# Second attention of a two-layer kernel: results of a batch carried by transfers into one array of full rows, divided once per batch, projected by one product per half

## The chip, the cores and the metric

The kernel runs on one core of a Trainium2 chip. A core has TensorE (PE, matrix products into PSUM), VectorE (DVE), ScalarE (ACT), GpSimd (POOL) and SyncE (SP), which in this kernel issues the transfers (DMAs); 16 DMA engines carry them. The metric is the time of one execution on the device in microseconds (us), as a median of several runs; lower is better.

## The reference

Two layers are computed on an input of 4 batches, 1024 tokens and 128 features: layer 0 (a scan, an attention, gated experts) and layer 1 (an attention over 16 heads of 8 features, then routed experts). The change touches the attention of layer 1 alone:

```python
h = NUM_HEAD                     # 16
hd = d_model // h                # 8
scale = jnp.sqrt(jnp.float32(h + D_KV + D_Q))      # 12
...
query = qt_c + qt_r
key = kt_c + kt_r
value = heads(ct_kv @ Wu_v_w + Wu_v_b)
attn = jnp.einsum('bhqd,bhkd->bhqk', query, key) / scale
attn = jax.nn.softmax(attn, axis=-1)
out = jnp.einsum('bhqk,bhkd->bhqd', attn, value)
out = out.transpose(0, 2, 1, 3).reshape(b, s, d_model)
return out @ Wo_w + Wo_b
```

## The kernel before, in words

The attention of layer 1 is the function `head_attention`; its tiles have names that begin with `h_`. It works in 16 groups n = 0 to 15 (`NGR`): 4 batches (`B`) of 4 groups (`NG`), and each group has 4 heads (`HG`). A group takes 16 steps i (`NI`): two halves of the 1024 queries (512 each, `CH`) by 8 tiles of 128 keys.

In a step TensorE makes two score tiles for two heads each (`scores`, line 1282, into `ps_st`), ScalarE takes their exponentials (`h_P`, line 1438), and one step later `values` (line 1292) multiplies them with the values into `ps_o`. The 4 heads of a group lie there at partitions 0, 32, 64 and 96; of each 32 partitions 9 are in use, 8 for the head's features and the ninth for the sum of the exponentials. `keep` (ScalarE, line 1404) copies each half to one of 7 arrays `o`.

The softmax needs each query's maximum. For it TensorE makes score tiles of another form in a ring of three PSUM banks (`maxima`, line 1266), two pairs of tiles a step and 24 pairs (12 steps) ahead of `scores`, and VectorE reduces each tile (line 1552): four reductions a step. After half a group the maxima are settled, GpSimd splits them into bf16 parts (`split`), TensorE turns them (`turn`, at steps 6 and 14), ScalarE keeps the turned rows (`h_m_row`, line 1397), and SP lays them beside the queries of the coming scores with four DMAs (`place_maxima`, line 1181). The scores of a half wait for these four (`m_landed`).

The division by the sums goes through memory. SP stores the four rows of sums (line 1186), loads them flat (1190), VectorE inverts them between two reductions (`invert`, line 1512), which falls at about step 8 of the group after, SP stores them (1194) and spreads each head's row over 32 partitions with four DMAs (line 1199, into `h_inv`). GpSimd multiplies `o` with `inv` (`norm`, line 1456), two instructions per group. When a batch's four groups are done, the output projection of its half c is four products accumulated over the groups (`output`, line 1249), with weights `h_Wo` padded with zeros for the 24 unused partitions of each head. These stand at step 2 of the third and fourth group of the next batch: two products ahead of the second pair of maxima of that step, two behind it. The last batch has its own way: sums spread by a product (line 1314), inverted on VectorE (1536, 1538), and `out_last` (line 1324), half 0 at step 13 of group 15, half 1 behind the last values.

SP is one queue in this order, for each n: `fetch_sums(n-1)`, `place_maxima(n, 1)`, in two groups of a batch `swap_rows`, then `spread_sums(n-1)`, in two groups of a batch `keep_parts` (768 KB of new keys or queries to memory), `load(n+2)` (12 DMAs of keys and queries, line 1754, 768 KB), and `place_maxima(n+1, 0)`. Between step 8 and step 14, groups n with n mod 4 of 0 or 1 also carry two products of the next batch's preparation (`product`, at steps 9 and 11); the others carry none. So `load` and the placing of the next group's maxima stand behind `spread_sums` on SP.

Of the kernel before, what the change touches and what calls it, by code (L numbers as in the profile page):

```python
# [1073 lines left out]
def head_weights(nc, ctx, S, A):  # L1074

    def sb(name, shape):
        return ctx.enter_context(nc.sbuf_tensor("h_" + name, shape, F32))

    W = S.head = State()
    W.Wd, W.bd, W.Wu, W.Wk, W.Wkv = sb("Wd", [D, 2, 64]), sb("bd", [128, 1]), sb("Wu", [64, 2, D]), sb("Wk", [D, D]), sb("Wkv", [128, 2, D])  # L1080
    W.Wo, W.bv, W.cos, W.sin = sb("Wo", [128, NG, D]), sb("bv", [128, NG]), sb("cos", [128, T]), sb("sin", [128, T])
    W.sums = sb("sums", [128, 128])
    W.loaded = semaphore(nc, ctx, "h_weights_loaded")
    W.count = 14


def load_head_weights(sp, S, A):

    W = S.head
    for to, x in ((W.Wd[:, 0, :], "Wd_q"), (W.Wd[:, 1, :], "Wd_kv"), (W.bd[0:64, :], "bd_q"), (W.bd[64:128, :], "bd_kv"),  # L1090
                  (W.Wu[:, 0, :], "Wq_r1"), (W.Wu[:, 1, :], "Wu_q"), (W.Wk[:, :], "Wk_r1"), (W.Wkv[64:128, 0, :], "Wu_k"), (W.Wkv[64:128, 1, :], "Wu_v"), (W.bv[:, :], "bvG"),
                  (W.cos[:, :], "cos1"), (W.sin[:, :], "sin1"), (W.sums[:, :], "sums_of")):
        sp.dma_start(to, A[x]).then_inc(W.loaded, 16)
    sp.dma_start(W.Wo[:, :, :], A["WoG1"].rearrange("p (g d) -> p g d", g=NG)).then_inc(W.loaded, 16)


def head_attention(nc, S, A):
# [8 lines left out]
    NB, PR, NBUF, NOB, NLOAD, MIX = 3, 4, 4, 7, 12, 16  # L1106
# [24 lines left out]
    with stage(nc) as ctx:  # L1131
        def sb(name, shape, dt=F32):
            return ctx.enter_context(nc.sbuf_tensor("h_" + name, shape, dt))

        def sem(name):
            return semaphore(nc, ctx, "h_" + name)
# [7 lines left out]
        o = [sb(f"o{i}", [128, T]) for i in range(NOB)]  # L1144
        inv = [sb(f"inv{i}", [128, T]) for i in range(2)]
# [75 lines left out]
        def _(pe):  # L1221
# [95 lines left out]
            def out_last(c, g0, g1):  # L1317
                for g in range(g0, g1):
                    n = (B - 1) * NG + g
                    if g == 0:  # L1320
                        pe.wait_ge(normed, 2 * (NGR - 1))
                    if g == NG - 1:
                        pe.wait_ge(normed_last, 2 * (c + 1))
                    last = pe.matmul(ps_max[:, 1 + c, :], Wo[:, g, :], o[n % NOB][:, c * CH:(c + 1) * CH], start=(g == 0), stop=(g == NG - 1))
                if g1 == NG:
                    last.then_inc(out_made, 1)

            pe.wait_ge(W.loaded, 16 * W.count)
            for g in range(NG):
                last = pe.matmul(ps_max[:, 0, 0:1], Wo[:, g, :], bv[:, g:g + 1], start=(g == 0), stop=(g == NG - 1))  # L1330
            last.then_inc(bias_made, 1)
# [8 lines left out]
            for n in range(NGR):  # L1340
                for i in range(NI):
# [12 lines left out]
                    if key and key[0] == "out":  # L1354
                        output(key, 0, NG // 2)
# [3 lines left out]
                    if key and key[0] == "out":  # L1359
                        output(key, NG // 2, NG)  # L1360
                    if n == NGR - 1 and i == KT + 1:
                        spread_last_sums(0)
                    if n == NGR - 1 and i == NI - 3:
                        out_last(0, 0, NG)
            values(NGR - 1, NI - 1)
            out_last(1, 0, 1)
            spread_last_sums(1)
            out_last(1, 1, NG)

        @block.scalar  # L1370
        def _(act):
# [79 lines left out]
        def _(pool):  # L1451
            def norm(n, c):
                cols = slice(c * CH, (c + 1) * CH)
                pool.wait_ge(inv_loaded, 16 * HG * (n + 1))
                pool.wait_ge(o_kept, 2 * n + 2)
                pool.tensor_tensor(o[n % NOB][:, cols], o[n % NOB][:, cols], inv[n % 2][:, cols], ALU.mult).then_inc(normed, 1)
# [21 lines left out]
            for n in range(NGR):  # L1478
# [3 lines left out]
                if n >= 2:  # L1482
                    for c in range(2):
                        norm(n - 2, c)
# [13 lines left out]
            for c in range(2):  # L1498
                norm(NGR - 2, c)

        @block.vector
        def _(dve):
# [1079 lines left out]
def layout(i):  # L2582
# [13 lines left out]
    def paired(a):  # L2596
# [30 lines left out]
        "Wu_k": paired(i["L1_attn_Wu_k_w"]), "Wu_v": i["L1_attn_Wu_v_w"], "bvG": beside(i["L1_attn_Wu_v_b"].reshape(NG, HG, 8), np.zeros((NG, HG, 24))).reshape(NG, 128).T,  # L2627
        "WoG1": beside(i["L1_attn_Wo_w"].reshape(NG, HG, 8 * D), np.zeros((NG, HG, 24 * D))).reshape(NG, 128, D).transpose(1, 0, 2).reshape(128, NG * D), "Wr": i["L1_ffn_Wr"], "b2": i["L1_ffn_b2"].reshape(1, X * D), "W1": i["L1_ffn_W1"], "W2": i["L1_ffn_W2"],
# [60 lines left out]
```

## Time and profile before

| | |
|---|---|
| median of 3 runs | 2175.93 us (2174.69 to 2179.72) |
| the profiled execution | 2174.7 us, its span 2172.9 us |
| busy over the span | PE 85%, DVE 67%, ACT 51%, POOL 31% |
| attention of layer 1, groups 0 to 15 | from about 1283 us to 1982 us of the span |

The busy shares are means over many stages; what a stage is bound by is read in that stage. In the timeline an entry merges equal instructions: the start, the time from the first start to the last end, the engine, the line, the operation, its tiles and shapes, the number of instructions, and in brackets the idle time ahead of it and what ended it. A product of f32 operands shows as two MATMUL entries, one of bf16 as one.

### The profile page before, as it was taken

Reading aid. Unit: us, or ns where it says so; the run is one execution under the profiler, and the core shown is the slowest. Engines: PE = TensorE matmul, PEld = TensorE weight load, DVE = VectorE, ACT = ScalarE, POOL = GpSimd, SP = SyncE. Lnnn points to the kernel's source line nnn. Section 1 sums busy time; section 2 is a strip of 40 time slices with the busy share of each in tenths; the row PEclk is TensorE's granted clock in tenths of the full one; section 3 lists DMA queues with packets and bytes.
Section 4 is the critical chain, followed back from the end, with each engine's and each line's share of the span. In section 5 each row is a group of like instructions: output and inputs, shape, how many; then the busy total and the mean of one; then the engine's idle time right before and its main releaser. Section 6 shows DMA issues by size and latency. Waiting matters only on the chain. (4 is left out here: it accounts for less than half of the span.)

```text
span 2172.9 us, 33046 instructions
## 1 busy us (share of the span) xinstructions
PE 1851.2 (85%) x12141; PEld 675.9 (31%) x12141; DVE 1464.0 (67%) x3100; ACT 1111.0 (51%) x1383; POOL 667.8 (31%) x804
## 2 busy tenths in 40 slices
PE   7454799999999999999499868888888888887879
PEld 3123233333333333333433312112211211113556
DVE  5864666666566566653344588999898899973443
ACT  4312244444444445444224248778777778774422
POOL 0032455544545465512025002403312511010052
PEclk9777799999999999999599969999999999998889
DMA  3000000000000000000021001101111111003114
GB/s 123 0 1 1 1 12 12 12 12 12 12 12 13 12 12 22 13 12 12 19 107 56 23 14 57 47 27 54 64 35 37 51 51 41 27 22 101 59 32 134
DMA packets 58229, 74.01 MB, mean 34 GB/s; under 512 B 23492, under 2 KB 39876, under 8 KB 57940
## 3 DMA queue, kind: packets, MB, share of 16 engines
q1 hardware_dynamic: 56500, 68.21, 10.0%
q0 software_dynamic: 1280, 2.62, 0.4%
q8 instruction: 98, 1.61, 0.3%
q10 hardware_dynamic: 288, 1.05, 0.2%
q14 instruction: 63, 0.52, 0.1%
HBM read 50.02 MB, written 16.98 MB: 31 GB/s over the span
## 5 line engine op out<-in xcount | busy, mean ns | idle before, releaser
L1552 DVE TENSOR_REDUCE h_m_half<-h_ps_max 128x1 f32<-128x512 f32 x1024 | 635.7, 683 | 66.7 <-PE h_ps_max L1266 64.2
L1438 ACT ACTIVATE h_P<-h_ps_st 128x1024 f32<-128x1024 f32 x512 | 496.9, 1022 | 93.1 <-PE h_ps_st L1282 90.3
L925 ACT ACTIVATE l_P<-l_ps_st 128x1024 f32<-128x1024 f32 (+3 forms) x384 | 306.8, 809 | 297.6 <-PE l_ps_st L808 296.5
L808 PE MATMUL l_ps_st<-l_Q,l_K 64*128 64x512 f32 (+3 forms) x1536 | 329.1, 509 | 0.4 <-DMA l_Q<-l_m_row 0.4
L1002 DVE CUSTOM_DVE_ANT_0 l_masked<-l_ps_t,l_mask 128x384 bf16<-128x384 f32 (+3 forms) x512 | 230.2, 487 | 83.0 <-PE l_ps_t L766 81.5
L1266 PE MATMUL h_ps_max<-h_K,h_Q 48*128 48x512 bf16 x1024 | 204.8, 396 | 91.7 <-DVE h_m_half L1552 89.9
L1292 PE MATMUL h_ps_o<-h_P,h_V 128*9 128x512 f32 x2048 | 269.2, 598 | 0.7 <-ACT h_P L1438 0.5
L1005 DVE TENSOR_REDUCE l_m_half<-l_ps_t 128x1 f32<-128x512 f32 x256 | 164.9, 686 | 100.6 <-PE l_ps_t L766 100.5
L973 POOL TENSOR_SCALAR_AFFINE_SELECT l_P<-l_P 128x256 f32<-128x256 f32 x256 | 103.2, 409 | 390.5 <-ACT l_P L925 390.0
L1282 PE MATMUL h_ps_st<-h_Q,h_K 51*128 51x512 bf16 x1024 | 169.3, 382 | 12.1 <-DMA h_Q<-h_m_row 4.9
L1469 POOL CAST h_m_parts<-h_m_neg 128x16 bf16<-128x16 f32 x32 | 6.3, 198 | 550.9 <-DVE h_m_neg L1529 550.9
L1266 PEld LDWEIGHTS h_ps_max<-h_K,h_Q 48*128 48x128 bf16 x1024 | 50.3, 93 | 399.6 <-DVE h_m_half L1552 376.5
L766 PE MATMUL l_ps_t<-l_Kh,l_Qh 64*128 64x512 bf16 (+3 forms) x768 | 129.7, 333 | 44.7 <-DVE l_m_half L1002 18.4
L823 PE MATMUL l_ps_o<-l_P,l_V 128*17 128x512 f32 (+3 forms) x1536 | 161.6, 493 | 6.2 <-POOL l_P L973 6.2
L808 PEld LDWEIGHTS l_ps_st<-l_Q,l_K 64*128 64x128 f32 x1536 | 127.4, 187 | 103.3 <-issue 46.8
L766 PE MATMUL l_ps_t<-l_Kl,l_Qh 64*128 64x512 bf16 (+3 forms) x768 | 128.0, 329 | 0.0
L766 PE MATMUL l_ps_t<-l_Kh,l_Ql 64*128 64x512 bf16 (+3 forms) x768 | 128.0, 329 | 0.0
L766 PEld LDWEIGHTS l_ps_t<-l_Kh,l_Qh 64*128 64x128 bf16 x768 | 37.6, 93 | 221.8 <-DVE l_m_half L1002 97.7
L944 POOL TENSOR_TENSOR l_t<-l_t,l_sin 128x512 f32<-128x512 f32 x72 | 92.3, 1282 | 37.8 <-DVE l_t L1023 37.8
L1022 DVE TENSOR_TENSOR l_t<-l_ps_t,l_cos 128x512 f32<-128x512 f32 x64 | 44.3, 691 | 66.2 <-PE l_ps_t L787 64.7
L950 POOL TENSOR_TENSOR l_Q<-l_t 128x512 f32<-128x512 f32 x64 | 81.8, 1278 | 8.4
L787 PE MATMUL l_ps_t<-xn,l_Wq 128*128 128x512 f32 x128 | 73.0, 654 | 4.2 <-DVE l_t L1023 4.2
(375 smaller groups left out, 2327.3 us busy)
## 6 DMA issues: line engine op xcount, KB each, us to landing
l_inv<-inverse_sums SPq DMA_DIRECT2D x60, 128.0 KB
h_inv<-inverse_sums SPq DMA_DIRECT2D x60, 128.0 KB, 2.8
y_rows<-zero SPq DMA_DIRECT2D x8, 512.0 KB, 4.9
h_b<-h_a SPq DMA_DIRECT2D x32, 128.0 KB, 2.0
c_W<-in_W SPq DMA_DIRECT2D x16, 256.0 KB, 5.6
c_back<-y_rows SPq DMA_DIRECT2D x16, 256.0 KB, 5.2
k_parts<-h_parts SPq DMA_DIRECT2D x4, 768.0 KB, 4.1
h_K<-k_parts SPq DMA_DIRECT2D x32, 96.0 KB
```

The costliest lines, as they stand in the source:

```text
L766: last = pe.matmul(tile(t + a)[:, 0:w], q[n % 2][rows, p, qt * 128:(qt + 1) * 128], k[n // NG % 2][rows, lo:lo + w], start=(x == 0), stop= ...
L808: last = pe.matmul(ps_st[x % 2][:, a, 0:w], K[n // NG % 2][rows, kt * 128:(kt + 1) * 128], Q[n % NQ][rows, c, p, q0 - c * CH:q0 - c * CH + ...
L823: last = pe.matmul(ps_o[32 * j:32 * j + M, q0 - c * CH:CH], V[n // NG][:, kt, :], P[(2 * (n * NI + i) + j // 2) % PR][:, j % 2, 0:w], star ...
L925: act.activation(P[e % PR][:, :, 0:w], ps_st[slot["s", n, i, p] % 2][:, :, 0:w], ACT.Exp, scale=0.125).then_inc(consumed, 1)
L973: pool.affine_select(P[e % PR][:, :, 0:128], P[e % PR][:, :, 0:128], [[0, 2], [1, 128]], ALU.is_ge, 0.0, base=0, channel_multiplier=-1).th ...
L1002: dve.tensor_tensor_reduce(out=masked[(t + a) % NB][:, 0:w], in0=ps, in1=mask[:, CH - w:CH], scale=-1.0, scalar=-NEG, op0=ALU.add, op1=ALU ...
L1005: dve.tensor_reduce(to, ps, AX.X, ALU.max, negate=True).then_inc(tile_freed, 1)
L1266: pe.matmul(ps_max[:, (t + a) % NB, :], Q[n % NBUF][rows, p, qt * 128:(qt + 1) * 128], K[n % NBUF][rows, p, lo:lo + CH], start=True, stop= ...
L1282: last = pe.matmul(to[:, a, :], K[n % NBUF][rows, p, kt * 128:(kt + 1) * 128], Q[n % NBUF][rows, p, c * CH:(c + 1) * CH], start=True, stop ...
L1292: last = pe.matmul(ps_o[32 * j:32 * j + M, :], V[b % 2][:, kt, g * HG + j, :], P[(2 * (n * NI + i) + j // 2) % PR][:, j % 2, :], start=(kt ...
L1438: act.activation(P[e % PR][:, :, :], ps_st[x % 2][:, :, :], ACT.Exp, scale=1.0 / 12.0).then_inc(consumed, 1)
L1552: dve.tensor_reduce(m_half[:, half, 2 * p + a, qt:qt + 1], ps_max[:, t % NB, :], AX.X, ALU.max, negate=True)\
```

## The change

A group's results are no longer divided where they stand. After the inverses of a group are stored, SP carries its 4 times 8 feature rows by four SBUF to SBUF DMAs into 32 rows of a new array `packed` (one of two, by the batch), which holds the 128 features of a whole batch in full rows; and it spreads each head's inverse over 8 partitions, not 32, at the same rows of `inv` (one per batch, no longer per group). GpSimd divides once per batch, two instructions, ahead of `split(2n+1)` in the second group of the batch after. The output projection of a half is one product of 128 full rows with the unpadded weights. Of the last batch the first three groups are divided that way (96 rows) and its fourth as before, so `out_last` has two products per half. Since `o` is free once it was carried, there are 4 arrays `o`, not 7; `keep` waits for the carries (`o_packed`) and for the stored sums of four groups back.

```diff
-    NB, PR, NBUF, NOB, NLOAD, MIX = 3, 4, 4, 7, 12, 16
+    NB, PR, NBUF, NOB, NLOAD, MIX = 3, 4, 4, 4, 12, 16
...
+        packed = [sb(f"packed{i}", [128, T]) for i in range(2)]
...
                 sp.wait_ge(inv_stored, 16 * (n + 1))
-                if n >= 2:
-                    sp.wait_ge(normed, 2 * (n - 1))
+                if n >= 2 * NG:
+                    sp.wait_ge(normed, 2 * (n // NG - 1))
+                    sp.wait_ge(consumed, item["out", n // NG - 2, 1] + 1)
+                if n:
+                    sp.wait_ge(o_packed, 16 * HG * n)
                 for j in range(HG):
-                    sp.dma_start(inv[n % 2][32 * j:32 * j + 32, :], inv1[n, j].partition_broadcast(32)).then_inc(inv_loaded, 16)
+                    at = 32 * (n % NG) + 8 * j
+                    sp.dma_start(packed[n // NG % 2][at:at + 8, :], o[n % NOB][32 * j:32 * j + 8, :]).then_inc(o_packed, 16)
+                for j in range(HG):
+                    at = 32 * (n % NG) + 8 * j
+                    sp.dma_start(inv[n // NG % 2][at:at + 8, :], inv1[n, j].partition_broadcast(8)).then_inc(inv_loaded, 16)
...
-            def output(key, g0, g1):
+            def output(key):
                 _, b, c = key
-                if g0 == 0:
-                    free_slot(item[key])
-                    pe.wait_ge(normed, 2 * NG * (b + 1))
-                for g in range(g0, g1):
-                    last = pe.matmul(ps_st[item[key] % 2][:, 0, :], Wo[:, g, :], o[(b * NG + g) % NOB][:, c * CH:(c + 1) * CH],
-                                     start=(g == 0), stop=(g == NG - 1))
-                if g1 == NG:
-                    last.then_inc(st_ready, 1)
+                to = free_slot(item[key])
+                pe.wait_ge(normed, 2 * (b + 1))
+                pe.matmul(to[:, 0, :], Wo[:, 0, :], packed[b % 2][:, c * CH:(c + 1) * CH], start=True, stop=True).then_inc(st_ready, 1)
...
+            def out_last(c, last):
+                cols = slice(c * CH, (c + 1) * CH)
+                if last:
+                    pe.wait_ge(normed_last, 2 * (c + 1))
+                    pe.matmul(ps_max[:, 1 + c, :], Wo[:, 1, :], o[(NGR - 1) % NOB][:, cols], start=False, stop=True).then_inc(out_made, 1)
+                else:
+                    pe.wait_ge(normed, 2 * B)
+                    pe.matmul(ps_max[:, 1 + c, :], Wo[0:96, 0, :], packed[(B - 1) % 2][0:96, cols], start=True, stop=False)
...
                 if n >= NOB:
-                    act.wait_ge(consumed, item["out", (n - NOB) // NG, 1] + 1)
+                    act.wait_ge(o_packed, 16 * HG * (n - NOB + 1))
+                    act.wait_ge(sums_stored, 16 * (n - NOB + 1))
...
-                if n >= 2:
+                if n % NG == 1 and n > NG:
                     for c in range(2):
-                        norm(n - 2, c)
+                        norm(n // NG - 1, c)
```

TensorE's queue at step 2 of a group that carries an `output`, before:

```order
L1292 MATMUL h_ps_o<-h_P,h_V 9x512 x4
L1249 MATMUL h_ps_st<-h_o,h_Wo 128x512 x2
L1266 MATMUL h_ps_max<-h_K,h_Q 128x512 x2
L1249 MATMUL h_ps_st<-h_o,h_Wo 128x512 x2
L1282 MATMUL h_ps_st<-h_Q,h_K 128x512 x2
L1266 MATMUL h_ps_max<-h_K,h_Q 128x512 x2
```

The same place in the changed program (the lines have moved by four):

```order
L1296 MATMUL h_ps_o<-h_P,h_V 9x512 x4
L1256 MATMUL h_ps_st<-h_packed,h_Wo 128x512
L1270 MATMUL h_ps_max<-h_K,h_Q 128x512 x2
L1286 MATMUL h_ps_st<-h_Q,h_K 128x512 x2
L1270 MATMUL h_ps_max<-h_K,h_Q 128x512 x2
```

Four products around a pair of maxima have become one product ahead of it. SP's queue in a group without `keep_parts`, from the store of the inverses on, before:

```order
L1194 DMA inverse_sums<-h_flat 128x32
L1199 DMA h_inv<-inverse_sums 32x1024 x4
L1754 DMA h_K<-k_parts 24x1x2048
L1754 DMA h_K<-k_parts 16x1x2048
L1754 DMA h_K<-k_parts 8x2048
...
L1181 DMA h_Q<-h_m_row 3x4x128 x4
```

And in the changed program:

```order
L1196 DMA inverse_sums<-h_flat 128x32
L1205 DMA h_packed<-h_o 8x1024 x4
L1208 DMA h_inv<-inverse_sums 8x1024 x4
L1755 DMA h_K<-k_parts 24x1x2048
L1755 DMA h_K<-k_parts 16x1x2048
L1755 DMA h_K<-k_parts 8x2048
...
L1183 DMA h_Q<-h_m_row 3x4x128 x4
```

Four DMAs now stand between the store of the inverses and the spread, so everything behind them, the 12 loads and the placing of the maxima, is issued four DMAs later.

## Rows read from the trace of the kernel before

**Rows 1.** Waits from 1290 to 1985 us: total in us, times, longest.

```profile
DVE h_m_half L1552 <- PE h_ps_max L1266: 52.0, 56, 1.9
...
PE h_ps_st L1282 <- DMA h_Q<-h_m_row: 4.9, 3, 2.0
```

**Rows 2.** VectorE's timeline at an output step (group 6, step 2).

```profile
1547.27 1.29 DVE L1552 TENSOR_REDUCE h_m_half<-h_ps_max 128x1 f32<-128x512 f32 x2 [1.90 <-PE h_ps_max L1266]
1549.72 1.29 DVE L1552 TENSOR_REDUCE h_m_half<-h_ps_max 128x1 f32<-128x512 f32 x2 [1.16 <-PE h_ps_max L1266]
1551.74 1.29 DVE L1552 TENSOR_REDUCE h_m_half<-h_ps_max 128x1 f32<-128x512 f32 x2 [0.73 <-PE h_ps_max L1266]
```

**Rows 3.** VectorE's timeline at a step with one product.

```profile
1304.56 2.48 DVE L1552 TENSOR_REDUCE h_m_half<-h_ps_max 128x1 f32<-128x512 f32 x4 [1.04 <-PE h_ps_max L1266]
1307.25 2.48 DVE L1552 TENSOR_REDUCE h_m_half<-h_ps_max 128x1 f32<-128x512 f32 x4 [0.20 <-PE h_ps_max L1266]
```

**Rows 4.** TensorE's timeline, one product (at 1303) and four (at 1544).

```profile
1303.08 1.13 PE L1233 MATMUL h_ps_st<-hT,h_Wd 128*128 128x512 f32 x2
...
1544.93 1.98 PE L1249 MATMUL h_ps_st<-h_o,h_Wo 128*128 128x512 f32 x4
```

**Rows 5.** Timeline of the last group, steps 8 to 14.

```profile
1955.86 2.50 POOL L1456 TENSOR_TENSOR h_o<-h_o,h_inv 128x512 f32<-128x512 f32 x2 [7.90 <-DMA h_inv<-inverse_sums]
...
1963.67 3.70 PE L1324 MATMUL h_ps_max<-h_o,h_Wo 128*128 128x512 f32 x8
...
1967.74 1.94 ACT L1438 ACTIVATE h_P<-h_ps_st 128x1024 f32<-128x1024 f32 x2 [3.58 <-PE h_ps_st L1282]
```

**Rows 6.** SP's timeline in group 7 (no product between steps 8 and 14).

```profile
1610.25 1.72 SPq L1199 DMA_DIRECT2D h_inv<-inverse_sums  x4
1612.07 3.77 SPq L1754 DMA_DIRECT2D h_K<-k_parts  x6
1615.88 3.68 SPq L1754 DMA_DIRECT2D h_Q<-q_parts  x6
1622.78 2.98 SPq L1181 DMA_DIRECT2D h_Q<-h_m_row  x4
```

**Rows 7.** SP's timeline in group 1 (two products between).

```profile
1349.11 4.41 SPq L1754 DMA_DIRECT2D h_K<-k_parts  x6
...
1361.30 3.01 SPq L1181 DMA_DIRECT2D h_Q<-h_m_row  x4
```

**Rows 8.** TensorE's timeline, first scores of groups 3 and 8.

```profile
1407.49 0.61 PE L1282 MATMUL h_ps_st<-h_Q,h_K 51*128 51x512 bf16 x4 [1.84 <-DMA h_Q<-h_m_row]
...
1627.06 0.60 PE L1282 MATMUL h_ps_st<-h_Q,h_K 51*128 51x512 bf16 x4
```

**Rows 9.** VectorE's timeline behind the wait of group 3.

```profile
1408.33 1.29 DVE L1552 TENSOR_REDUCE h_m_half<-h_ps_max 128x1 f32<-128x512 f32 x2 [1.36 <-PE h_ps_max L1266]
1410.38 2.68 DVE L1552 TENSOR_REDUCE h_m_half<-h_ps_max 128x1 f32<-128x512 f32 x4 [0.76 <-PE h_ps_max L1266]
```

**Rows 10.** Windows: time, PE, PEld, DVE, ACT, POOL busy, TensorE clock, DMA share, GB/s.

```profile
1390.00:1395.00 5.00, 4.30 (x36) 0.85 (x32) 5.00 (x9) 3.92 (x5) 0.00 (x0) 1.00 0.87 270
...
1406.40:1406.80 0.40, 0.00 (x0) 0.00 (x0) 0.40 (x1) 0.00 (x0) 0.00 (x0) 1.00 0.00 0
1408.00:1410.00 2.00, 2.00 (x14) 0.25 (x12) 1.29 (x2) 2.00 (x3) 0.00 (x0) 0.66 0.00 0
1614.00:1622.00 8.00, 6.88 (x54) 1.38 (x50) 7.96 (x15) 6.28 (x7) 2.97 (x6) 1.00 0.21 78
1625.40:1625.80 0.40, 0.27 (x2) 0.10 (x2) 0.40 (x2) 0.40 (x1) 0.00 (x0) 1.00 0.04 8
```

**Rows 11.** DMA issues on SP: count, duration ns min/median/max (three queries).

```profile
L1199 SPq DMA_DIRECT2D h_inv<-inverse_sums x60: 322/421/432, 1346.9 to 1952.8; - x60
...
L1703 SPq DMA_DIRECT2D h_b<-h_a x24: 517/591/1078, 1297.1 to 1695.4; - x24
...
L715 SPq DMA_DIRECT2D l_Q<-l_m_row x64: 634/641/823, 230.2 to 998.6; - x64
```

More of the change, by code:

```diff
@@ L1080, in head_weights @@
     W.Wd, W.bd, W.Wu, W.Wk, W.Wkv = sb("Wd", [D, 2, 64]), sb("bd", [128, 1]), sb("Wu", [64, 2, D]), sb("Wk", [D, D]), sb("Wkv", [128, 2, D])
-    W.Wo, W.bv, W.cos, W.sin = sb("Wo", [128, NG, D]), sb("bv", [128, NG]), sb("cos", [128, T]), sb("sin", [128, T])
+    W.Wo, W.bv, W.cos, W.sin = sb("Wo", [128, 2, D]), sb("bv", [128, 1]), sb("cos", [128, T]), sb("sin", [128, T])
     W.sums = sb("sums", [128, 128])
@@ L1093, in load_head_weights @@
         sp.dma_start(to, A[x]).then_inc(W.loaded, 16)
-    sp.dma_start(W.Wo[:, :, :], A["WoG1"].rearrange("p (g d) -> p g d", g=NG)).then_inc(W.loaded, 16)
+    sp.dma_start(W.Wo[:, :, :], A["WoG1"].rearrange("p (g d) -> p g d", g=2)).then_inc(W.loaded, 16)
 def head_attention(nc, S, A):
@@ L1166, in head_attention @@
         inv_stored, inv_loaded, normed, joined = sem("inv_stored"), sem("inv_loaded"), sem("normed"), sem("joined")
+        o_packed = sem("o_packed")
         block = ctx.enter_context(nc.Block())
@@ L1315, in spread_last_sums @@
                   .then_inc(spread_last, 1)
[L1317 to L1326, printed above, removed]
+            def out_last(c, last):
[6 more added lines that the diff above has]
+                    pe.matmul(ps_max[:, 1 + c, :], Wo[0:96, 0, :], packed[(B - 1) % 2][0:96, cols], start=True, stop=False)
             pe.wait_ge(W.loaded, 16 * W.count)
-            for g in range(NG):
-                last = pe.matmul(ps_max[:, 0, 0:1], Wo[:, g, :], bv[:, g:g + 1], start=(g == 0), stop=(g == NG - 1))
-            last.then_inc(bias_made, 1)
+            pe.matmul(ps_max[:, 0, 0:1], Wo[:, 0, :], bv[:, 0:1], start=True, stop=True).then_inc(bias_made, 1)
             pe.wait_ge(cleared, 1 + 2)
@@ L1354, in _ @@
                     if key and key[0] == "out":
-                        output(key, 0, NG // 2)
+                        output(key)
                     elif key:
@@ L1358, in _ @@
                     maxima(n + (s + 1) // NPAIR, (s + 1) % NPAIR)
-                    if key and key[0] == "out":
-                        output(key, NG // 2, NG)
                     if n == NGR - 1 and i == KT + 1:
@@ L1363, in _ @@
                     if n == NGR - 1 and i == NI - 3:
-                        out_last(0, 0, NG)
+                        out_last(0, False)
+                        out_last(0, True)
             values(NGR - 1, NI - 1)
-            out_last(1, 0, 1)
+            out_last(1, False)
             spread_last_sums(1)
-            out_last(1, 1, NG)
+            out_last(1, True)
         @block.scalar
@@ L1451, in _, with norm @@
         def _(pool):
[L1452 to L1456, printed above, removed]
+            def norm(b, c):
+                cols, hi = slice(c * CH, (c + 1) * CH), 128 if b < B - 1 else 96
+                groups = hi // 32 + NG * b
+                pool.wait_ge(inv_loaded, 16 * HG * groups)
+                pool.wait_ge(o_packed, 16 * HG * groups)
+                pool.tensor_tensor(packed[b % 2][0:hi, cols], packed[b % 2][0:hi, cols], inv[b % 2][0:hi, cols], ALU.mult).then_inc(normed, 1)
             def join(b):
@@ L1498, in _ @@
             for c in range(2):
-                norm(NGR - 2, c)
+                norm(B - 1, c)
         @block.vector
@@ L1534, in divide_last @@
                 if c == 0:
-                    dve.wait_ge(normed, 2 * (NGR - 2))
-                dve.reciprocal(inv[n % 2][:, cols], ps_max[:, 0, :]).then_inc(normed_last, 1)
+                    dve.wait_ge(normed, 2 * (B - 1))
+                dve.reciprocal(inv[B % 2][:, cols], ps_max[:, 0, :]).then_inc(normed_last, 1)
                 dve.wait_ge(normed_last, 2 * c + 1)
-                dve.tensor_tensor(o[n % NOB][:, cols], o[n % NOB][:, cols], inv[n % 2][:, cols], ALU.mult).then_inc(normed_last, 1)
+                dve.tensor_tensor(o[n % NOB][:, cols], o[n % NOB][:, cols], inv[B % 2][:, cols], ALU.mult).then_inc(normed_last, 1)
             def join_last(c):
@@ L2626, in layout @@
         "Wk_r1": paired(i["L1_attn_Wk_r_w"]),
-        "Wu_k": paired(i["L1_attn_Wu_k_w"]), "Wu_v": i["L1_attn_Wu_v_w"], "bvG": beside(i["L1_attn_Wu_v_b"].reshape(NG, HG, 8), np.zeros((NG, HG, 24))).reshape(NG, 128).T,
-        "WoG1": beside(i["L1_attn_Wo_w"].reshape(NG, HG, 8 * D), np.zeros((NG, HG, 24 * D))).reshape(NG, 128, D).transpose(1, 0, 2).reshape(128, NG * D), "Wr": i["L1_ffn_Wr"], "b2": i["L1_ffn_b2"].reshape(1, X * D), "W1": i["L1_ffn_W1"], "W2": i["L1_ffn_W2"],
+        "Wu_k": paired(i["L1_attn_Wu_k_w"]), "Wu_v": i["L1_attn_Wu_v_w"], "bvG": i["L1_attn_Wu_v_b"].reshape(D, 1),
+        "WoG1": beside(i["L1_attn_Wo_w"], beside(i["L1_attn_Wo_w"][96:].reshape(HG, 8 * D), np.zeros((HG, 24 * D))).reshape(128, D)), "Wr": i["L1_ffn_Wr"], "b2": i["L1_ffn_b2"].reshape(1, X * D), "W1": i["L1_ffn_W1"], "W2": i["L1_ffn_W2"],
         "fw1": i["L1_ffn_fw1"], "fw2": i["L1_ffn_fw2"],
```

## The prediction

> **What bounds the kernel now.** I read the waits of this attention first. VectorE waits for score tiles 52.0 us in 56 places, and TensorE waits 3 times, 4.9 us in all and at most 2.0, for the turned maxima that SP lays beside the queries [rows 1]. In ordinary steps VectorE never idles: its four reductions set the step, 2.48 us (the four in one row of [rows 3]). So TensorE's work costs only where it holds VectorE up, and SP's only where its DMAs land later than the scores want them. Its idles stand at the inserted products and behind those three waits. The timeline of VectorE shows an output step: 1.90 + 1.16 + 0.73 = 3.79 us [rows 2]. There are six (three batches, two halves), 22.7 of the 52.0 us. A step with one product ahead of its second maxima costs 1.04 + 0.20 = 1.24 us [rows 3].
>
> **What the output products give back.** TensorE's timeline has two products in 1.98 us before and again behind the maxima, and 1.13 us for a lone one [rows 4]. The change leaves one, at the place of the lone product of [rows 3]. So an output step should idle VectorE as that one does: 3.79 - 1.24 = 2.55 us less, six times 15.3 us. Bounds: if the 0.20 falls away, 16.5; TensorE itself loses three of four products, 3 x 1.98/2 = 3.0 us, so at most 17.8. I take 15.3. The eviction of the result is unchanged.
>
> In the last group four products of half 0 stand in ScalarE's way: 3.70 us of TensorE and 3.58 us of idle ScalarE [rows 5]. Two are left, 1.85 us saved, all of it from a wait that stays above it: 1.8 us. Of half 1 the removed products stood behind the last sums and in front of VectorE's division, in cover. Together **17.1 us** gained.
>
> **GpSimd** loses 22 of 30 divisions, each half of the pair in 2.50 us [rows 5]. It is off the path: nothing. At the end the division must still precede TensorE's products at 1963.67; it began at 1955.86 and comes about 2.6 us later (below), ends at 1961.0, and is covered by 2.7 us. Without that cover the excess would be paid once. The new waits find their work done: ScalarE's `keep` asks for carries issued some three groups earlier, SP for those of the group before, and GpSimd divides a batch whose last inverses landed in the group before. Less weight to load and a smaller bias product: nothing.
>
> **What SP pays.** Four DMAs are added ahead of the 12 loads and of `place_maxima`. The spreads shrink from 128 to 32 KB each, but an issue's time does not follow the bytes: a spread takes 421 ns, an 8-row DMA of half a KB per row between two SBUF arrays 641 ns, one of 32 rows of 4 KB between SBUF arrays 591 ns [rows 11]. The carry, SBUF to SBUF with 8 rows of 4 KB, is not in the trace. Lowest, as a spread plus a gap of some 0.05 us, four cost 1.9 us; highest, as the 641 ns, 2.8. I take the 591 ns: 4 x 0.64 = 2.55, and 0.05 for waits: the loads start **2.6 us later** in every group that spreads and loads (n = 1 to 13).
>
> Is that hidden? In group 7 the loads are issued from 1612.07 to 1619.56, then SP waits for the turned rows until 1622.78 [rows 6], so SP itself has 3.2 us to spare. The DMA engines have less. From 1614 to 1622 the load moves 78 GB/s at a share of 0.21, that is three or four of 16 engines, and its last packets are seen at 1625.4 to 1625.8 [rows 10], 6 us after SP issued the last. So it is bound by those engines from its start, and shifts with it. The four small DMAs of the maxima are queued behind. In group 2 the load's traffic ended by about 1406.4 [rows 10] and the first scores of group 3 began at 1407.49, after 1.84 us of waiting [rows 8]: about 1.0 us from end of load to scores. In group 7 the load ends near 1625.6 and the scores begin unhindered at 1627.06 [rows 8]: 1.46, less the 1.0, leaves a slack of about 0.4 us. A wait of TensorE reaches VectorE less 0.5 us (1.84 became 1.36) [rows 8, 9].
>
> - Groups 3, 7, 11, 12, 13 carry no product between steps 8 and 14 and store no parts: wait 2.6 - 0.4 = 2.2, VectorE idles 1.7, together 8.5 us.
> - Groups 2, 6, 10 wait already. Their loads stand behind a store of 768 KB and the spreads, which fill the engines to 0.87 at 270 GB/s [rows 10]. The change takes 4 x (128 - 2 x 32) = 256 KB out of that, worth 1.0 us. So 1.6 us more each, 4.8 us.
> - Groups 1, 5, 9 have two products between, which give the load 12.19 us until the maxima's DMAs in place of 10.71 [rows 6, 7], but also a store of 768 KB. Slack 0.9 to 1.9; about 0.5 us of idle each, 1.5 us.
> - Groups 4, 8 have the products and no store: slack 1.9 and more, nothing. Group 14 loads nothing.
>
> Then the clock. After the wait of group 3 the granted TensorE clock was 0.66 of full over 2 us [rows 10], part of it at 1.2 and part at 2.4 GHz, and VectorE idled another 0.76 us [rows 9]. With 8 to 11 waits, I count three more such events, 2.5 us.
>
> Loss: 8.5 + 4.8 + 1.5 + 2.5 = **17.3 us**. Sum against the profiled 2174.7 us: -17.1 + 17.3 = +0.2. The profile stands 1.2 us under the median of the runs; I forecast 2175.0 us. The bounds move the loss: a shift of 1.9 us makes it 5 x 1.0 + 3 x 0.9 + 0 + 1 = 9, net -8; a shift of 2.9 us, with no relief from the smaller spreads and 5 us for the clock, 5 x 2.0 + 3 x 2.9 + 2.4 + 5 = 26, net +9. A change under 0.2%, 4.4 us, can hardly be told from none.
>
> **The rivals.**
>
> *The carries are hidden.* Nothing of the 17.3 us is paid, and the kernel takes 2175.9 - 17.1 = 2158.8 us. For it: 3.2 us of SP's own slack [rows 6], and only three waits now [rows 1]. Against it: load traffic that outlasts its issue by 6 us and a slack of 0.4 us. The Trainium skill ("DMA: Bandwidth & Descriptors", "Issuing engines are not separate DMA queues") calls the time of an issue usually small relative to the DMA itself; by that rule the carries would hardly delay the queue, and this rival would hold. The rows have 0.6 us of issue for such a DMA, and four stand in a row, so I do not follow it.
>
> *The delay is shorter than I take it.* A carry issues like a spread, or the slack is nearer 1 us. Then the loss is 5 to 10 us: 2166 to 2171, about 2168.
>
> *The waits cost the clock each time: slower.* TensorE waits 2 to 3.5 us at the head of 8 to 11 groups, and each is followed by a stretch like that of group 3, in which the maxima come late. At 0.8 us for each of 11, and no relief for groups 2, 6 and 10, the loss is 8.5 + 7.8 + 1.5 + 8.8 = 26.6 and the time 2175.9 + 9.5 = 2185; half-way 2181. It decides for slower once the waits and the clock lose over 21.5 us. For it: one of three waits did so. Against it: the longest of the three was 2.0 us [rows 1], and only that of group 3 has a second idle behind it in VectorE's timeline.
>
> *The change does not do what it says* I leave out: the products are counted in the program's order.
>
> **How the numbers follow.** Forecast within 0.2%: 0.43. Shorter delay: 0.20. Hidden: 0.12. Slower: 0.25. So faster 0.32, same 0.43, slower 0.25. The range leaves out the hidden case and the far end of the slower one: 2165 to 2183. The likeliest case's own range is 2171.6 to 2180.3.
>
> **What the next profile would show.** VectorE's idle at an output step near 1.2 us, not 3.79; ScalarE's idle in the last group near 1.7, not 3.58. Four carries in 2.3 to 2.8 us on SP, and the first load 4.4 us behind the first carry. TensorE waiting for the turned maxima about 11 times, 20 us or more in all, near 2.2 us in groups 3, 7, 11, 12, 13 (they show at the first scores of the group behind). I am wrong if carries issue in under 0.5 us, if the load's end does not move with its start, or if output steps still idle over 2 us.

## The result, and the profile after

The changed kernel takes 2188.8 us (median of 4 runs, 2185.82 to 2191.36) and the kernel before 2175.31 us (2174.6 to 2179.72, 4 runs): a ratio of 1.0055 with a 95% interval of 1.0037 to 1.0072. It is slower, by 13.5 us between the medians. The profiled execution has a span of 2184.1 us where that of before had 2172.9, 11.2 us more. All spans of the attention below are of profiled executions.

The waits from 1290 to 1985 us, total in us, times, longest, to be laid beside [rows 1]:

```profile
DVE h_m_half L1553 <- PE h_ps_max L1270: 67.1, 67, 4.2
...
PE h_ps_st L1286 <- DMA h_Q<-h_m_row: 27.2, 12, 4.0
```

VectorE idles 15.1 us more than before, and TensorE waits for the turned maxima 12 times, 27.2 us, where it waited 3 times, 4.9 us. Both halves of the forecast's sum are in these two lines. The timeline of VectorE at an output step (group 6, step 2) and of ScalarE in the last group has the gain:

```profile
1551.77 2.48 DVE L1553 TENSOR_REDUCE h_m_half<-h_ps_max 128x1 f32<-128x512 f32 x4 [1.04 <-PE h_ps_max L1270]
1554.45 1.29 DVE L1553 TENSOR_REDUCE h_m_half<-h_ps_max 128x1 f32<-128x512 f32 x2 [0.21 <-PE h_ps_max L1270]
...
1979.01 3.77 ACT L1438 ACTIVATE h_P<-h_ps_st 128x1024 f32<-128x1024 f32 x4 [1.87 <-PE h_ps_st L1286]
```

The output step idles 1.04 + 0.21 = 1.25 us, where [rows 2] had 3.79. In the last group ScalarE idles 1.87 us for the 3.58 of [rows 5].

SP's timeline in group 7, to be laid beside [rows 6], and in group 2, shows what was paid for it:

```profile
1605.47 2.98 SPq L1183 DMA_DIRECT2D h_Q<-h_m_row  x4
1611.53 0.35 SPq L1196 DMA_DIRECT2D inverse_sums<-h_flat  x1
1612.97 3.10 SPq L1205 DMA_DIRECT2D h_packed<-h_o  x4
1616.12 1.54 SPq L1208 DMA_DIRECT2D h_inv<-inverse_sums  x4
1617.77 3.81 SPq L1755 DMA_DIRECT2D h_K<-k_parts  x6
1621.62 3.69 SPq L1755 DMA_DIRECT2D h_Q<-q_parts  x6
1625.49 2.99 SPq L1183 DMA_DIRECT2D h_Q<-h_m_row  x4
...
1391.81 4.29 SPq L1755 DMA_DIRECT2D h_K<-k_parts  x6
```

From the start of what follows the stored inverses to the first load SP needs 1617.77 - 1612.97 = 4.80 us; before it was 1612.07 - 1610.25 = 1.82. The load is 2.98 us later in its group, which is more than in most: read in the same way, it is 2.5 to 2.6 us in ten of the thirteen groups that load, 3.0 in groups 7 and 8, and 1.4 in group 6. SP's 3.2 us of slack ahead of the turned rows are gone: the load's issue ends at 1625.31 and the maxima follow at 1625.49. Only four DMAs of 8 rows were added, of 32 KB each.

What the scores make of that stands in TensorE's timeline, the first scores of groups 2, 3, 4, 8 and 11 (in brackets the wait):

```profile
1364.41 0.61 PE L1286 MATMUL h_ps_st<-h_Q,h_K 51*128 51x512 bf16 x4 [1.66 <-DMA h_Q<-h_m_row]
1408.01 1.04 PE L1286 MATMUL h_ps_st<-h_Q,h_K 51*128 51x512 bf16 x4 [4.03 <-DMA h_Q<-h_m_row]
1451.94 1.04 PE L1286 MATMUL h_ps_st<-h_Q,h_K 51*128 51x512 bf16 x4 [2.01 <-DMA h_Q<-h_m_row]
...
1632.87 1.04 PE L1286 MATMUL h_ps_st<-h_Q,h_K 51*128 51x512 bf16 x4 [2.94 <-DMA h_Q<-h_m_row]
...
1770.54 1.04 PE L1286 MATMUL h_ps_st<-h_Q,h_K 51*128 51x512 bf16 x4 [3.52 <-DMA h_Q<-h_m_row]
```

All twelve waits stand at the heads of groups. That of group 9 is 0.15 us and is left out of what follows, so eleven remain. And in four of the five rows the four products behind the wait take 1.04 us, where the same four took 0.61 before [rows 8]. The windows tell why (columns as in [rows 10]; the clock is the number ahead of the DMA share), and VectorE's timeline behind the wait of group 3 shows what it costs (compare [rows 9]):

```profile
1408.00:1410.00 2.00, 1.99 (x10) 0.44 (x14) 0.52 (x1) 1.34 (x2) 0.00 (x0) 0.50 0.00 0
1410.00:1412.00 2.00, 2.00 (x12) 0.29 (x6) 0.90 (x3) 1.19 (x2) 0.00 (x0) 0.50 0.00 0
1412.00:1414.00 2.00, 2.00 (x14) 0.23 (x10) 1.90 (x4) 1.69 (x2) 0.00 (x0) 0.50 0.03 8
1414.00:1416.00 2.00, 1.65 (x16) 0.31 (x8) 1.56 (x3) 1.03 (x2) 0.00 (x0) 0.98 0.05 8
```

```profile
1409.48 1.29 DVE L1553 TENSOR_REDUCE h_m_half<-h_ps_max 128x1 f32<-128x512 f32 x2 [4.18 <-PE h_ps_max L1270]
1411.87 2.68 DVE L1553 TENSOR_REDUCE h_m_half<-h_ps_max 128x1 f32<-128x512 f32 x4 [1.10 <-PE h_ps_max L1270]
1414.99 5.63 DVE L1553 TENSOR_REDUCE h_m_half<-h_ps_max 128x1 f32<-128x512 f32 x9 [0.44 <-PE h_ps_max L1270]
```

Behind the wait at the head of group 3 TensorE ran at 0.50 of full, the level of 1.2 GHz, for six microseconds, and was busy all of that time. VectorE idled 4.18 us, not 4.03 less 0.5, and then 1.10 and 0.44 us more. Such stretches come with eight of the eleven waits. By windows of 2 us the clock is low for 3.4 us in five of them and for 6.8 us in the other three.

### The profile page after: what moved, and what is told of

Same layout as the page of the kernel before. It is cut to its first block and busy times, and to the rows that moved or that the text cites. A ratio compares the mean times of both kernels' runs of the same rounds, so it can differ in the third digit from the quotient of the medians.

```text
span 2184.1 us, 32976 instructions
## 1 busy us (share of the span) xinstructions
PE 1842.6 (84%) x12091; PEld 667.5 (31%) x12091; DVE 1464.4 (67%) x3100; ACT 1111.5 (51%) x1383; POOL 639.6 (29%) x782
## 3 DMA queue, kind: packets, MB, share of 16 engines
q0 software_dynamic: 1280, 2.62, 0.4%
## 5 line engine op out<-in xcount | busy, mean ns | idle before, releaser
L1296 PE MATMUL h_ps_o<-h_P,h_V 128*9 128x512 f32 x2048 | 276.0, 612 | 0.7 <-ACT h_P L1438 0.5
L1286 PE MATMUL h_ps_st<-h_Q,h_K 51*128 51x512 bf16 x1024 | 173.1, 391 | 32.4 <-DMA h_Q<-h_m_row 27.2
L1286 PEld LDWEIGHTS h_ps_st<-h_Q,h_K 51*128 51x128 bf16 x1024 | 50.7, 96 | 94.1 <-issue 34.0
```

The source lines that it names most:

```text
L1286: last = pe.matmul(to[:, a, :], K[n % NBUF][rows, p, kt * 128:(kt + 1) * 128], Q[n % NBUF][rows, p, c * CH:(c + 1) * CH], start=True, stop ...
L1296: last = pe.matmul(ps_o[32 * j:32 * j + M, :], V[b % 2][:, kt, g * HG + j, :], P[(2 * (n * NI + i) + j // 2) % PR][:, j % 2, :], start=(kt ...
```

## The experiments

The kernels of the first, second and fourth part below, and that with four idle DMAs, ran on a chip where the kernel before took 2176.88 us; the others ran on chips where it took 2167.99 us and, for the last kernel, 2167.6. So ratios are compared, and absolute times only within one group. "VectorE's idle" is the first line above, "TensorE's waits" the second, over the same 1290 to 1985 us.

**One product per half, without the carries.** Of `output` in the kernel before, only the first of four products per half is left; three of a batch's four groups are missing in its result.

```diff
-                for g in range(g0, g1):
-                    last = pe.matmul(ps_st[item[key] % 2][:, 0, :], Wo[:, g, :], ...
-                if g1 == NG:
-                    last.then_inc(st_ready, 1)
+                if g0 == 0:
+                    pe.matmul(ps_st[item[key] % 2][:, 0, :], Wo[:, 0, :], ...,
+                              start=True, stop=True).then_inc(st_ready, 1)
```

> The kernel before with one product in place of four in the six output steps of batches 0 to 2 (three of the four groups of heads are left out of the projection, so the output is incomplete); all else as before. Theory A: VectorE idles 1.2 us at each such step and not 3.8, and six times 2.55 us come off whole: 2175.3 - 15.3 = 2160 us. If the gain of these steps were taken back elsewhere in the stage (ScalarE or the waits for the maxima): 2170 to 2175 us.

Measured: 2160.49 us, ratio 0.9924 (0.9899 to 0.9948). VectorE's idle is 35.5 us where [rows 1] has 52.0, 16.5 less, and the time fell by 16.4. About 1 us of that is not theirs, since TensorE's three waits are shorter here (3.3 us for 4.9). The gain of the six output steps is real, and of the size forecast (15.3).

**The carries ahead of SP's wait for the inverses.** In the changed kernel the carries and their waits, which need only `o` and `packed`, move up from behind the stored inverses; nothing else differs.

```diff
             def spread_sums(n):
+                if n >= 2 * NG:
+                    sp.wait_ge(normed, 2 * (n // NG - 1))
+                    sp.wait_ge(consumed, item["out", n // NG - 2, 1] + 1)
+                if n:
+                    sp.wait_ge(o_packed, 16 * HG * n)
+                for j in range(HG):
+                    at = 32 * (n % NG) + 8 * j
+                    sp.dma_start(packed[n // NG % 2][at:at + 8, :], o[n % NOB][32 * j:32 * j + 8, :]).then_inc(o_packed, 16)
                 sp.wait_ge(inverted, n + 1)
                 sp.dma_start(inv1[n]...).then_inc(inv_stored, 16)
                 sp.wait_ge(inv_stored, 16 * (n + 1))
...
```

> The changed kernel with the four carries issued ahead of SP's wait for the inverses, where SP stands idle for about 3.0 us in the kernel before; spreads and loads keep their order behind. Theory A (the cost is the place of the carries on SP: they delay the load by 3.0 us, the turned maxima land behind it and TensorE waits 27 us and loses its clock): the first load starts again about 1.7 us behind the first spread, TensorE waits at most as in the kernel before (3 times, 5 us), and the time is 2188.8 minus about 28 to 30, 2159 to 2161 us. Rival B (the cost is in the carries themselves, wherever they stand: more small transfers, the fewer arrays of results, the waits of ScalarE for them): 2185 to 2190 us.

Measured: 2159.56 us, ratio 0.992 (0.9901 to 0.994), 17.3 us below before. VectorE's idle is 35.8 us. TensorE's waits are 7.9 us in 9 places, more than I had expected, but none is over 1.2 us and the clock stays at 1.00 behind all of them. SP's timeline in group 7 shows where the carries went, and then that of group 1:

```profile
1593.77 2.96 SPq L1183 DMA_DIRECT2D h_Q<-h_m_row  x4
1596.78 2.76 SPq L1202 DMA_DIRECT2D h_packed<-h_o  x4
1599.82 0.35 SPq L1204 DMA_DIRECT2D inverse_sums<-h_flat  x1
1601.50 1.29 SPq L1208 DMA_DIRECT2D h_inv<-inverse_sums  x4
1603.23 3.80 SPq L1755 DMA_DIRECT2D h_K<-k_parts  x6
...
1340.13 2.44 SPq L1704 DMA_DIRECT2D h_b<-h_a  x4
1342.61 2.78 SPq L1202 DMA_DIRECT2D h_packed<-h_o  x4
1345.44 0.45 SPq L1204 DMA_DIRECT2D inverse_sums<-h_flat  x1
```

In group 7 they lie in the time in which SP waits for the inverses (from 1608.45 to 1611.53 in the changed kernel, 3.1 us), and the load starts 1.73 us behind the first spread. In groups 1, 4, 5, 8 and 9 SP has the four DMAs of `swap_rows` to issue first, and little of that time is left: measured from the first scores of group 1, the inverses are stored at 26.4 us, and at 24.2 in the two other kernels. The products of these groups give their loads more time, and the waits behind them stay at 0.5 to 1.2 us or nothing. All transfers of the change are still made, so it is their place on SP that cost 29 us, not they.

**The delay without the change.** In the kernel before, four (and in another kernel two) DMAs of 8 rows of 4 KB between SBUF arrays stand where the carries would, into an array that nothing reads.

```diff
                     sp.wait_ge(normed, 2 * (n - 1))
+                if n:
+                    sp.wait_ge(o_packed, 16 * 4 * n)
+                for j in range(4):
+                    sp.dma_start(spare[...8 rows], flat_rows[32 * j:32 * j + 8, :]).then_inc(o_packed, 16)
                 for j in range(HG):
                     sp.dma_start(inv[n % 2][32 * j:32 * j + 32, :], ...)
```

> The kernel before with four more DMAs per group at the place of the carries, SBUF to SBUF, 8 rows of 4 KB, whose data nobody uses; spreads of 32 partitions, seven arrays and the four products stay. Theory A: loads start about 2.7 to 2.9 us later, TensorE waits 24 to 28 us for the turned maxima in 11 groups, with half the clock behind most waits, and the time is 2175.3 + 26 to 32, 2201 to 2207 us. Rival B (the cost comes with the packed layout and its waits): 2175 to 2180 us.

Measured for four: 2212.27 us, ratio 1.0158 (1.0135 to 1.018), 35.4 us more. VectorE's idle is 84.2 us, TensorE's waits 30.6. That is above the upper end of what I had expected. VectorE loses 32.2 us where TensorE's waits grew by 25.7, so here too more is lost than was waited.

> The kernel before with two further DMAs per group, not four, at the place of the carries (data that nobody uses). They delay the load by about 1.4 us. Theory A with a slack of 0.4 to 0.5 us in groups 3, 7, 11, 12, 13 and 0.9 to 1.5 in groups 1, 5, 9: TensorE waits 4.9 + 3 x 1.4 + 5 x 0.95 + 0.5, about 14 us; VectorE loses 4 to 5 us more without the clock, 6 to 10 with it: 2182 to 2186 us, clearly under half of the 35 us that four cost. Rival C (each added DMA costs the same, whatever the slack): 2193 us.

Measured for two: 2179.14 us, ratio 1.0054 (1.0033 to 1.0076), 11.2 us more, again a little above. VectorE's idle is 63.4 us and TensorE's waits 16.1. Two DMAs cost a third of what four cost: a part of the first delay falls into slack. The clock was low behind three waits here and behind eight with four DMAs, so the cost does not grow in proportion. The loss of the changed kernel comes from the four DMAs at that place and needs nothing else of the change.

**The clock alone.** In the changed kernel TensorE makes sixteen small products, into the score tile that the coming scores then overwrite, in front of the wait for the turned maxima in ten groups. SP and every wait stay.

```diff
+    WAITS = (2, 3, 4, 7, 8, 10, 11, 12, 13, 14)
...
                 if kt == 0 and p == 0:
+                    if c == 0 and n in WAITS:
+                        for k in range(16):
+                            rows = slice(64 * (k % 2), 64 * (k % 2) + D6)
+                            pe.matmul(to[:, k % 2, :], K[n % NBUF][rows, 0, 0:128], Q[n % NBUF][rows, 0, 0:CH], start=True, stop=True)
                     pe.wait_ge(m_landed[c], 16 * HG * (n + 1))
```

> The changed kernel with 16 products without use (their tiles are overwritten by the scores) ahead of TensorE's wait for the turned maxima, in the ten groups where it waits over 1 us; some 1.8 us of work each at full clock. Theory A1 (of the 30 us that the waits cost VectorE, some 13 come from the clock, which stands at 0.50 for 2 to 6 us behind a wait): the clock stays at 1.00 behind the waits, VectorE's second and third idles vanish, and the time falls by 8 to 13 us to 2176 to 2181 us. Rival A2 (those idles come from TensorE's queue catching up after a wait, at whatever clock): 2187 to 2192 us.

Measured: 2178.87 us, ratio 1.0012 (0.9997 to 1.0027), against 1.0055 of the changed kernel: some 9 us back. TensorE's and VectorE's timelines at the head of group 3, then two windows:

```profile
1403.97 1.89 PE L1287 MATMUL h_ps_st<-h_Q,h_K 48*128 48x512 bf16 x16
1408.50 0.61 PE L1291 MATMUL h_ps_st<-h_Q,h_K 51*128 51x512 bf16 x4 [2.64 <-DMA h_Q<-h_m_row]
...
1409.36 10.00 DVE L1558 TENSOR_REDUCE h_m_half<-h_ps_max 128x1 f32<-128x512 f32 x16 [3.90 <-PE h_ps_max L1271]
...
1409.00:1411.00 2.00, 1.92 (x18) 0.31 (x14) 1.64 (x3) 2.00 (x3) 0.00 (x0) 1.00 0.00 0
...
1766.00:1768.00 2.00, 2.00 (x12) 0.28 (x6) 0.98 (x2) 1.65 (x3) 0.00 (x0) 0.50 0.00 0
```

The wait itself is no shorter: 1.89 + 2.64 = 4.53 us from the last other product to the scores, where the changed kernel had 4.03. But the clock stands at 1.00, the scores behind the wait take 0.61 us, and sixteen reductions follow without a gap. VectorE's idle is 55.7 us, 11.4 less than in the changed kernel. At the head of group 11, the second window, the clock fell all the same, to 0.50. So of the loss, some 9 to 11 us are the clock's; the waits keep the rest.

**The loads ahead of the whole division.** `spread_sums(n - 1)`, carries and all, moves behind the loads and the next group's maxima, in the changed kernel and in the kernel before.

```diff
-                if n:
-                    spread_sums(n - 1)
...
                 if n + 2 < NGR:
                     load(n + 2)
                 if n + 1 < NGR:
                     place_maxima(n + 1, 0)
+                if n:
+                    spread_sums(n - 1)
```

> The changed kernel with the store of parts, the 12 loads and the placing of the turned maxima ahead of the whole handling of the inverses on SP (carries and spreads last in the group). Theory A: no load is late, TensorE waits for the turned maxima under 1 us in all, VectorE idles only at inserted products, about 32 us: 2188.8 minus 33 to 35, 2154 to 2157 us. If the division, now some 15 us later, became late for the output products or the arrays of results were not free in time, TensorE or ScalarE would wait there and the time would stay over 2160 us.

> The kernel before with the same move: loads and turned maxima ahead of the handling of the inverses, nothing else. Theory A: its three waits of 4.9 us and VectorE's 4.4 us behind them go, 2175.9 - 4.4 = about 2171.5 us; the order of SP's queue alone is worth no more than this before the carries come. If more hangs on the order than these waits: under 2168 us.

Measured: the changed kernel with the move takes 2142.37 us, ratio 0.9887 (0.9864 to 0.991), 25.6 us below before on the same chip; the kernel before with the move takes 2161.47, ratio 0.9974 (0.996 to 0.9988). That is 6.5 us below before, where I had expected 4.4, which the interval allows; its VectorE's idle is 48.7 us, 3.3 less than before, so a part of the 6.5 is not explained. The change on top of the move is worth 19.1 us, close to the 17.1 of its output products. The waits of the first of the two:

```profile
POOL h_packed L1457 <- DMA h_inv<-inverse_sums: 50.8, 4, 13.8
...
DVE h_m_half L1553 <- PE h_ps_max L1270: 32.4, 45, 1.0
...
PE h_ps_st L1286 <- DMA h_Q<-h_m_row: 0.9, 2, 0.6
```

TensorE no longer waits for the maxima. The wait has gone to GpSimd, 50.8 us in four places, where it costs nothing: the division of a batch is not wanted before the third group. This is the fastest version of the study.

**The same DMAs once more, at either place.** A second set of four, into an array that nothing reads, behind the early carries (first) and behind those that stand after the loads (second).

```diff
+                if n:
+                    sp.wait_ge(again, 16 * HG * n)
+                for j in range(HG):
+                    at = 32 * (n % NG) + 8 * j
+                    sp.dma_start(spare[at:at + 8, :], W.cos[32 * j:32 * j + 8, :]).then_inc(again, 16)
```

> The version with the carries ahead of the wait for the inverses, with the four carries made a second time behind them into an array nobody reads: eight DMAs where SP has about 3 us of idle. Theory A (the early carries are free because they fill that idle): the first four fill it, the second four delay the load by about 2.7 us, and most of the loss returns, 2159.6 + 20 to 28, 2180 to 2188 us. Rival D (early carries are free wherever SP has passed the first maxima, since the transfers are small): 2160 to 2164 us.

> Everything is as in e2_loads_first (parts, loads and maxima of the next group ahead of the carries and spreads on SP), but a second set of four carries of the same size goes into an array that nothing reads, behind the first set. e2_loads_first took 0.9887 of the kernel before, and four issues of such carries on SP take about 2.8 us a group (rows of e2: 1612.85 2.75). Theory, the place on SP counts and not the number of transfers: SP has the time, since nothing that TensorE waits for stands behind them, so the ratio stays at 0.989 to 0.991, VectorE's idle time behind TensorE stays at 35 to 38 us, and TensorE's waits for Q stay under 3 us. Rival, each added set of four costs what it cost in e7_early_twice (over 20 us) wherever it stands: ratio 1.000 or more, VectorE's idle time over 55 us. Between the two: the second set delays the inverses' spreads and with them GpSimd's divisions, which could reach the one-product steps: then VectorE idles longer in front of them than e2's 1.04 us.

Measured: behind the early carries 2194.88 us, ratio 1.0131 (1.0106 to 1.0157), where one set gave 0.992: 2.1% or some 45 us for four more DMAs, where I had expected 20 to 28. Behind the loads 2144.77 us, ratio 0.9893 (0.9873 to 0.9913), where one set gave 0.9887. SP's timeline in group 7 of the one kernel, and then of the other:

```profile
1615.88 2.76 SPq L1202 DMA_DIRECT2D h_packed<-h_o  x4
1618.68 2.62 SPq L1207 DMA_DIRECT2D h_spare<-h_cos  x4
...
1624.59 3.81 SPq L1761 DMA_DIRECT2D h_K<-k_parts  x6
```

```profile
1614.40 2.97 SPq L1183 DMA_DIRECT2D h_Q<-h_m_row  x4
...
1618.96 2.73 SPq L1205 DMA_DIRECT2D h_packed<-h_o  x4
1621.74 3.61 SPq L1210 DMA_DIRECT2D h_spare<-h_cos  x4
```

In the first the early carries have used up the time until the inverses come, so the second set delays the store of the inverses and with it the load: TensorE waits in 13 places, 35.2 us, and VectorE idles 76.1 us, 40 more than with one set. The groups with `swap_rows` have no such time at all: the waits behind groups 1, 4, 5, 8 and 9 are 3.21, 1.94, 3.17, 2.60 and 3.44 us, together 14.4, where one set gave 3.4. In the second kernel the set takes 3.61 us, and VectorE idles 33.4 us for 32.4. The same four transfers cost some 45 us at the one place and, within the intervals, nothing at the other. VectorE's 40 us account for most of the 45.

## Why the prediction was wrong

**The gain was right.** Forecast 15.3 us at the output steps and 1.8 in the last group. Measured 6 x (3.79 - 1.25) = 15.2 and 3.58 - 1.87 = 1.7. The version without carries gave 16.4, the one with early carries 17.3. GpSimd's division was covered, as taken.

**The shift was right.** "The loads start 2.6 us later" came out as 2.5 to 2.6 in ten of thirteen groups, from two errors that cancel: four carries mostly take 2.73 to 2.81 us, not 2.55 (a single one has a median of 649 ns, close to the 641 ns that I kept as the upper end and not the 591 that I took), and the four spreads, smaller now, issue in 1.48 us, not 1.72.

**The waits came where the forecast put them.** For the loads of groups 3, 7, 11, 12 and 13 it said 2.2 us each. They stand at the first scores one group on: 2.01, 2.94, 2.33, 2.14 and 1.81, a mean of 2.25. For groups 2, 6 and 10 it said 1.6 more than before; they are 4.03, 3.31 and 3.52. The first went from 1.84 to 4.03, 2.2 more; together less 0.5 each they cost 6.0 us more than before, not 4.8. The relief of 1.0 us from the smaller spreads hardly came. Windows of 0.4 us show when the traffic of the load of group 2 and of the maxima behind it ends, after and then before:

```profile
1406.40:1406.80 0.40, 0.00 (x0) 0.00 (x0) 0.00 (x0) 0.00 (x0) 0.00 (x0) 1.00 0.05 15
1406.80:1407.20 0.40, 0.00 (x0) 0.00 (x0) 0.00 (x0) 0.00 (x0) 0.00 (x0) 1.00 0.03 5
```

```profile
1406.00:1406.40 0.40, 0.00 (x0) 0.00 (x0) 0.40 (x2) 0.00 (x0) 0.00 (x0) 1.00 0.08 21
```

The packets of under 512 bytes at the very end (all eleven of 1406.8 to 1407.2) are not the load's, whose packets of data are 4 KB each. The last of those ends at 1406.16 before, 15.2 us behind the load's first issue at 1391.00, and at 1406.68 after, 14.9 us behind 1391.81. In groups 6 and 10 the load's own duration shrank by 0.1 us. So taking 256 KB off the engines shortened these loads by 0.1 to 0.3 us, not by 1.0, as if they were bound by their few engines from the start. In each of the three groups the wait grew by the shift less this gain: in group 2 by 2.5 - 0.3 = 2.2 us. The maxima of group 2 were issued 1.3 us earlier than before (1399.89 for 1401.21), and still landed later. So it is the traffic, not SP, that holds them. The same reading puts the end of the load of group 7 before at 1625.2, not at the 1625.4 to 1625.8 of the forecast, which are packets of the maxima; the slack changes little by it.

The Trainium skill ("DMA: Bandwidth & Descriptors", "Why a DMA increments its semaphore by 16 and not by 1") says that a transfer issued from SP uses as many engines as the largest number up to 16 that divides the slowest dimension of both its sides, and takes the lowest-numbered. In `load` that dimension is 3 or 2 in the source of the larger transfers, so by that rule they run on 3 or 2 engines, whatever else the others do; the share of 0.21 of [rows 10], three or four of 16, agrees, and no run here shows which engines they are.

For groups 1, 5 and 9 it said 0.5 us each, and their waits are 1.66, 0.82 and 2.48: 1.65 in the mean, 1.15 less the 0.5 that does not reach VectorE. That is 3.5 us, not 1.5.

**The step that failed is the clock: "I count three more such events, 2.5 us".** The forecast had it too rare and too cheap. Where TensorE barely waits at all, with the loads first, VectorE's idle is 32.4 us. So the waits and what follows them cost 67.1 - 32.4 = 34.7 us in the changed kernel and 52.0 - 15.2 - 32.4 = 4.4 us before: a loss of 30.3 us, not 17.3. Of the 34.7 the waits themselves, 27.05 us at eleven heads of groups less 0.5 each, are 21.5, and the other 13.2 us lie in the stretches behind them in which TensorE runs at 1.2 GHz. Of the 4.4 before, 4.9 less three times 0.5, or 3.4, were waits, and 1.0 the clock. So the waits lost 18.1 us, where the forecast had 8.5 + 4.8 + 1.5 = 14.8, and the clock 12.2, where it had 2.5. The split is made by that 0.5, and two things bear it out. Behind the three waits that kept the clock, 1.66, 0.82 and 2.48 us, VectorE idled 1.18, 0.34 and 2.00, which is the wait less 0.48. And the filler gave 11.4 us of VectorE's time and some 9 us of the kernel's back, with the waits left in place.

Both factors of the term were off. The clock fell eight times where it had fallen once, so seven more events and not three. And an event costs 13.2 / 8 = 1.65 us in the mean, not the 0.8 that I took. The same reckoning gives 1.5 us an event in the kernels with two and with four idle DMAs (3 and 8 events) and in that with the early carries made twice (10). I had priced an event by the second idle of group 3 before, 0.76 us [rows 9]. That stretch was not shorter than most: the window behind the one in [rows 10] reads 0.50 throughout,

```profile
1410.00:1412.00 2.00, 2.00 (x12) 0.39 (x12) 1.52 (x3) 1.64 (x3) 0.00 (x0) 0.50 0.03 8
```

and the whole stretch 3.4 us. But there the clock fell 1.2 us behind the first scores. After, it did so only in group 12, where VectorE's second idle is 0.76 us again. In six of the other seven it fell while TensorE was still waiting, so the first scores already ran slowly, and three of the stretches were twice as long. Group 3 alone idles 0.65 (4.18 less 3.53) + 1.10 + 0.44 = 2.2 us for it. The rival named "the waits cost the clock each time" had the mechanism, and its price, 8.8 us, was still too low.

**The sum.** 30.3 us lost at the waits, less 15.2 at the output steps and 1.7 in the last group, is +13.4 us, against +11.2 of the profiled spans and +13.5 between the medians. Of the difference to the spans, 3.0 us lie ahead of 1290 us. VectorE's first reduction of the attention came at 1230.06 and before at 1232.14, and at about 1280 us it idled 1.84 us for 3.08. Neither is the change's: the kernels before with idle DMAs or with the move have the same program up to there, start between 1229.9 and 1234.5, and idle 1.69 to 3.08. The stretch behind the last reduction also varies, from 221 to 233 us among kernels whose program is that of before there. So that the account closes to 1 us is partly luck.

**The other rivals fall.** "The carries are hidden" is refuted by the early carries, which are 29 us faster with the same transfers. The Trainium skill ("DMA: Bandwidth & Descriptors", "Issuing engines are not separate DMA queues") calls the time of an issue usually small relative to the DMA. No run here contradicts that of a single DMA, but what was to follow from it, that the carries hardly delay the queue, is contradicted: four issues, 2.7 us in all, made the kernel lose its whole gain and more, since SP is one queue and a load of 13 to 15 us stands behind them. The measurement decides. "The delay is shorter than I take it" is refuted by 2.5 us in most groups.

## What to carry to other kernels

A queue that issues transfers is an engine with a timeline: before something is put into it, ask what stands behind it and whether that is late already, and put what is wanted late behind what is wanted early. Price a new wait of TensorE in a stage that it is nearly filling twice, for itself and for the slower clock behind it, which here was another 60% of what the waits themselves cost. Read the windows behind such a stretch to its end: the first of them alone hid more than half of it here. Where only the order on a queue spoils a change, changing the order tells the gain and the loss apart: the same change went from 1.0055 to 0.9887.

## What the runs showed of the hardware

- In the changed kernel the granted clock fell to 0.50 during or just behind waits of 4.03, 3.52, 3.31, 2.94, 2.33, 2.14, 2.01 and 1.81 us, and stayed at 1.00 behind waits of 2.48, 1.66 and 0.82. The length of the wait alone does not tell: one of 2.48 kept the clock and one of 1.81 lost it. Sixteen products of 1.89 us in all, directly ahead of the wait, kept it in nine of the ten groups that had them, where without them it was kept in two of the ten.
- A stretch at 0.50 lasted 3.4 or 6.8 us and cost VectorE 1.65 us in the mean. In it four score products take 1.04 us and not 0.61, and TensorE is busy throughout while VectorE, which else sets the pace, idles: the engine that bounds the stage changes for as long as the clock is low.
- The issue of an SBUF to SBUF transfer of 8 rows of 4 KB takes 649 ns on SP in the median of 60, and that of 8 rows spread from memory 295 ns, where 32 rows took 421 [rows 11]. The issue does not follow the bytes.
- Two added DMAs at the critical place cost 11 us, four 35 us, and a second set of four behind the loads nothing that can be told from noise.
